# Sparse attention and a mixture-of-experts block on one core: scores and maxima in units of two heads

## The reference

```python
qkv = layernorm(x) @ w_qkv                  # 2 x 1024 x 384
q, k, v = heads(qkv)                        # 2 batches x 16 heads, 1024 x 8
s = q @ k.T / sqrt(8), -inf where key > query
att = softmax(s) @ v                        # then @ w_o, residual, layernorm, experts
```

## Time and profile before

| | us |
|---|---|
| median of 3 runs | 2053.17 (2050.89 to 2055.31) |
| the profiled execution's own span | 2056.6 |
| TensorE (PE) busy in it | 1720.3 (84%) |
| PE weight loads busy | 999.4 (49%) |
| VectorE (DVE) busy | 1287.6 (63%) |
| ScalarE (ACT) busy | 1111.6 (54%) |
| GpSimd (POOL) busy | 548.3 (27%) |

### The profile page before, as it was taken

One profiled execution on the slowest core, in us unless ns is written; L12 is line 12 of the kernel. 1 busy time (PEld: TensorE's weight loads), 2 busy tenths in 40 slices (PEclk: granted clock), 3 DMA queues, 4 the chain that ended last, 5 costly groups with the idle time before them and its releaser, 6 DMA issues.

```text
span 2056.6 us, 33763 instructions
## 1 busy us (share of the span) xinstructions
PE 1720.3 (84%) x10588; PEld 999.4 (49%) x10588; DVE 1287.6 (63%) x3053; ACT 1111.6 (54%) x2328; POOL 548.3 (27%) x479
## 2 busy tenths in 40 slices
PE   3799999699967357888987978989489999969995
PEld 1344444477754114454654545556234444447774
DVE  5677775577785665464555645533467777557777
ACT  3367777388845343434344334323237767738883
POOL 6000000000001504786656867662500000000000
PEclk9699999699987566777567768567769999969998
DMA  4111110012102142101021111120211111002110
GB/s 132 64 49 50 48 46 9 27 66 83 51 2 88 62 110 49 42 28 50 28 63 46 29 46 31 43 64 18 92 62 49 50 50 44 9 30 85 61 52 21
DMA packets 66504, 104.26 MB, mean 51 GB/s; under 512 B 19432, under 2 KB 37296, under 8 KB 63280
## 3 DMA queue, kind: packets, MB, share of 16 engines
q1 hardware_dynamic: 56720, 84.86, 12.8%
q0 software_dynamic: 8192, 16.79, 2.8%
q10 hardware_dynamic: 1456, 0.90, 0.2%
HBM read 74.80 MB, written 8.59 MB: 41 GB/s over the span
## 4 chain that ended last, share of the span: by engine, by line
PE 58%; POOL 13%; issue 10%; DVE 8%; ACT 4%; SPq 3%; DVEq 2%; DMA 1%; ACTq 0%; another core or an unknown queue 0%; POOLq 0%
PE bank L701 10%; PE bank L847 8%; PE bank L685 7%; POOL onehot L639 7%; POOL arena L620 6%; PE bank L660 6%; PE bank L837 6%; PE bank L1001 2%; PE bank L1014 2%; ACT experts L1146 1%; PE bank L662 1%; PE bank L687 1%; PE bank L1029 1%; DVE arena L1313 1%; PE bank L1017 1%
## 5 line engine op out<-in xcount | busy, mean ns | idle before, releaser
L1313 DVE TENSOR_REDUCE arena<-bank 128x1 f32<-128x512 f32 (+3 forms) x768 | 382.9, 551 | 170.1 <-PE bank L662 117.3
L1073 ACT ACTIVATE arena<-bank 128x512 f32<-128x512 f32 (+3 forms) x768 | 335.2, 493 | 144.3 <-PE bank L687 121.5
L566 POOL TENSOR_TENSOR rstd<-vareps,neghalf 128x8 f32<-128x8 f32 x14 | 23.8, 1698 | 1168.0 <-DVE vareps L1306 1168.0
L660 PE MATMUL bank<-arena 72*128 72x512 bf16 (+3 forms) x768 | 259.8, 346 | 39.1 <-DMA arena<-arena 37.0
L620 POOL DMA_INDIRECT arena<-kv_rows,IDX x256 | 250.8, 980 | 155.9 <-ACT IDX L1242 86.7
L685 PE MATMUL bank<-arena 99*128 99x512 bf16 (+3 forms) x768 | 254.4, 335 | 6.0 <-ACT arena L1079 4.3
L639 POOL TENSOR_SCALAR onehot<-XT,const 128x512 fp32r<-128x512 f16 x136 | 212.4, 1573 | 160.7 <-DMA XT<-idx_rows 76.7
L701 PE MATMUL bank<-arena 128*32 128x512 f32 (+3 forms) x1536 | 225.4, 501 | 0.0
L1683 DVE TENSOR_TENSOR HN<-bank,RT 96x512 f32<-96x512 f32 x128 | 87.3, 682 | 206.8 <-PE bank L1001 144.2
L1371 DVE TENSOR_TENSOR experts<-arena,experts 128x512 fp32r<-128x512 f32 x256 | 171.6, 689 | 71.1 <-ACT experts L1146 71.1
L1144 ACT ACTIVATE arena<-bank,bias 128x512 f32<-128x512 f32 x256 | 185.6, 725 | 46.1 <-PE bank L837 46.0
(11 more groups left out here) (247 smaller groups left out, 2592.0 us busy)
## 6 DMA issues: line engine op xcount, KB each, us to landing
arena<-wt_rows SPq DMA_DIRECT2D x16, 1024.0 KB, 4.7
arena<-q_rows SPq DMA_DIRECT2D x192, 48.0 KB
arena<-k_rows SPq DMA_DIRECT2D x192, 48.0 KB
arena<-in_L_ffn_w SPq DMA_DIRECT2D x32, 256.0 KB, 5.1
arena<-arena SPq DMA_DIRECT2D x32, 256.0 KB
XT<-idx_rows SPq DMA_DIRECT2D x8, 1024.0 KB, 4.7
arena<-kv_rows,IDX POOLq DMA_INDIRECT x256
arena<-HN SPq DMA_DIRECT2D x32, 128.0 KB, 2.4
```

Of the source, the lines that this page charges most:

```text
L660: m = pe.matmul(o[:, 0:hi - lo], QB[buf][s][0:ROWS, qt * P:(qt + 1) * P], KB[buf][s][0:ROWS, lo:hi], start=True, stop=True)
L1073: act.activation(PT[w % PT_RING][:, 0:m], bank[S_RING + w % S_RING][:, 0:m], ACT.Exp, scale=float(HD) ** -0.5)\
L1313: dve.tensor_reduce(rowmax[:, hf, s, qt:qt + 1], bank[u % S_RING][:, 0:n], AX_X, ALU.max).then_inc(max_done, 1)
```

## The change

[...] Both heads of a pair lie in one tile, head 0 in rows 0 to 34 and head 1 in rows 64 to 98, and each matmul over them is one of two, in TensorE's two row halves, into two adjoining PSUM banks (`twin`). A unit is two heads by 512 columns; 9 units make a pass where 24 did. To fill 512 columns, several blocks share a unit (`PASS1`, `PASS2`): four of the maxima units and three of the scores units have one piece, two of the maxima units are four diagonal blocks, masked by one matmul of 512 columns a head, and the others have two pieces. A maximum and an exponential are one instruction over 2 x 512 columns. Maxima of pieces go to `partial` and one more reduction joins them.

Query tiles stand in the order 0, 3, 4, 7, 1, 2, 5, 6, so that each query half has 18 blocks; the values run in 5 groups instead of 8. Scores units and maxima units alternate over one ring of three twins (banks 0 to 5): a scores unit waits for the maxima unit two before it, a maxima unit for the exponential of the unit before it. Pass 1 is for the pair two ahead. PT has 6 buffers of 1024 columns. The q and k split is one ScalarE copy and one VectorE subtraction a block. A pair's rows come by 11 DMAs (4 KB rows) instead of 13, a row of zeros among them through DRAM; GpSimd makes the two masks and clears less.

The core of the diff (behind the first part only added and unchanged lines; what they replace is in the listing above):

```diff
-NPROD = 3 * 3
+PARTS = 2
 STRIP = 32
-ROWS = NPROD * HD
-MAXROW = 96
+TILE = 64
+PRODS = PARTS * PARTS * HD
 MAXROWS = 3
+ROWS = PRODS + MAXROWS
 RING = 4
...
+QORDER = [0, 3, 4, 7, 1, 2, 5, 6]
+QPLACE = [QORDER.index(t) for t in range(TB)]
+MORDER = [0, 2, 3, 1, 4, 6, 7, 5]
+MPLACE = [MORDER.index(t) for t in range(TB)]
+MSLOTS = 5
+PASS1 = [[(4, 0, 4)], [(5, 0, 4)], [(6, 0, 4)], [(7, 0, 4)], [(3, 0, 3), (1, 0, 1)], [(7, 4, 3), (5, 4, 1)], [(2, 0, 2), (6, 4, 2)],
+         [(t, t, 1) for t in MORDER[:4]], [(t, t, 1) for t in MORDER[4:]]]
+PASS2 = [[(0, 0)], [(1, 0)], [(1, 1)], [(0, 1), (0, 7)], [(0, 2), (0, 5)], [(1, 2), (1, 6)], [(0, 3), (0, 6)], [(1, 3), (1, 5)],
+         [(0, 4), (1, 4)]]
+UNITS = len(PASS1)
+GROUPS = [(0, 1), (2, 3), (4, 5), (6, 7), (8,)]
+GROUP_OF = [g for u in range(UNITS) for g, us in enumerate(GROUPS) if u in us]
+EARLY = 4
+HALFWAY = 5
 S_RING = 3
+PT_RING = 6
+TOTAL = UNITS * PAIRS
+def first_block(g, kc):
+    return [t >= kc for t in QORDER[4 * g:4 * g + 4]].index(True)
+def places(u):
+    at, out = 0, []
+    for g, kc in PASS2[u]:
+        p = first_block(g, kc)
+        out.append((g, kc, p, at))
+        at += 4 - p
+    assert at == 4
+    return out
+def diagonals(u):
+    return [at for g, kc, p, at in places(u) if QORDER[4 * g + p] == kc]
+ROW_LOADS = 16 * (2 * (2 * PARTS + 1) + 1)
...
+        twin = [ctx.enter_context(nc.psum_tensor(f"twin{i}", [P, 2 * BANK], F32)) for i in range(4)]
+        bank = [twin[i // 2][:, i % 2 * BANK:(i % 2 + 1) * BANK] for i in range(8)]
...
+        mask_qk = sb("mask_qk_b", [P, 4, P], BF16)
+        mask_kq = sb("mask_kq_b", [P, 2, P], BF16)
...
+        qparts = view("ffn", (PARTS, TOK), F32R)
+        kparts = view("ffn", (PARTS, TOK), F32R)
...
+        QB = [view("ffn", (L,), F32R) for i in range(RING)]
+        KB = [view("ffn", (L,), F32R) for i in range(RING)]
...
+        PT = [view("ffn", (2, BANK)) for i in range(PT_RING)]
+        partial = view("ffn", (2, TB, MSLOTS))
+        rowmax = view("ffn", (2, TB))
...
+                sp.wait_ge(pv_done, PV0 + len(GROUPS) * (g + it - RING + 1))
             for s in range(2):
+                q, k = (rows[it, s] if isinstance(it, int) else rows[bass.ds(it, 1), s].rearrange("a d r t -> (a d) r t") for rows in (q_rows, k_rows))
+                for i in range(PARTS):
+                    r = TILE * s + i * PARTS * HD
+                    sp.dma_start(QB[buf][r:r + PARTS * HD, :].bitcast(F32), q[:, i, :].unsqueeze(0).broadcast_to([PARTS, HD, L]))\
+                      .then_inc(rows_loaded[buf], 16)
+                    sp.dma_start(KB[buf][r:r + PARTS * HD, :].bitcast(F32), k.rearrange("d r t -> r d t")).then_inc(rows_loaded[buf], 16)
+                sp.dma_start(QB[buf][TILE * s + PRODS:TILE * s + ROWS, :].bitcast(F32), zero_rows).then_inc(rows_loaded[buf], 16)
...
+        def pe_pass1(pe, c, it, buf, u, visit, slot):
             n = PAIRS * c + it
             if u == 0:
                 pe.wait_ge(rows_loaded[buf], ROW_LOADS * (PAIRS // RING * c + visit + 1))
+            at = 0
+            for j, (qt, k0, blocks) in enumerate(PASS1[u]):
+                for s in range(2):
+                    r = slice(TILE * s, TILE * s + ROWS)
+                    q = QPLACE[qt]
+                    m = pe.matmul(bank[2 * slot + s][:, at * P:(at + blocks) * P], QB[buf][r, q * P:(q + 1) * P],
+                                  KB[buf][r, k0 * P:(k0 + blocks) * P], start=(j == 0), stop=True, skip_group_check=True)
+                at += blocks
+            if PASS1[u][0][0] == PASS1[u][0][1]:
+                for s in range(2):
+                    m = pe.matmul(bank[2 * slot + s][:, :], ident_b[:, :], mask_qk[:, :, :].rearrange("p a q -> p (a q)"),
+                                  start=False, stop=True, skip_group_check=True)
             m.then_inc(s1_done, 1)
...
+        def pe_scores(pe, c, it, buf, u, left):
             n = PAIRS * c + it
+            m = UNITS * it + u
+            if u == 0:
                 pe.wait_ge(maxrow_ready, 2 * n + 2)
+            if left >= 2:
+                pe.wait_ge(max_done, MAX0 + TOTAL * c + m + UNITS + EARLY - 1)
+            else:
+                pe.wait_ge(max_done, MAX0 + TOTAL * c + min(m + UNITS + EARLY - 1, TOTAL))
+                pe.wait_ge(exp_done, EXP0 + TOTAL * c + m - S_RING + 1)
+            slot = 2 * u % S_RING
+            for j, (g, kc, p, at) in enumerate(places(u)):
+                for s in range(2):
+                    r = slice(TILE * s, TILE * s + ROWS)
+                    x = pe.matmul(bank[2 * slot + s][:, at * P:(at + 4 - p) * P], KB[buf][r, kc * P:(kc + 1) * P],
+                                  QB[buf][r, (4 * g + p) * P:(4 * g + 4) * P], start=(j == 0), stop=True, skip_group_check=True)
+            at = diagonals(u)
+            if at:
+                for s in range(2):
+                    cut = bank[2 * slot + s][:, :].rearrange("p (t q) -> p t q", q=P)[:, at[0]:at[-1] + 1:max(1, at[-1] - at[0]), :]
+                    x = pe.matmul(cut, ident_b[:, :], mask_kq[:, 0:len(at), :], start=False, stop=True, skip_group_check=True)
+            x.then_inc(st_done, 1)
+        def pe_next(pe, c, it, buf, m, u, visit):
+            pe.wait_ge(exp_done, EXP0 + TOTAL * c + m)
+            pe_pass1(pe, c, it, buf, u, visit, (2 * ((u + HALFWAY) % UNITS) + 1) % S_RING)
...
+            for u in GROUPS[group]:
+                for g, kc, p, at in places(u):
+                    for s in range(2):
+                        r = (2 * s + g) * STRIP
+                        m = pe.matmul(bank[6][r:r + STRIP, p * P:], VS[buf][:, s, kc, :],
+                                      PT[(UNITS * buf + u) % PT_RING][:, s, at * P:(at + 4 - p) * P], start=(kc == 0), stop=True,
+                                      skip_group_check=True)
             m.then_inc(pv_done, 1)
...
+            two, one = (buf + 2) % RING, (buf + 1) % RING
+            for u in range(HALFWAY, UNITS):
+                pe_scores(pe, c, it, buf, u, left)
+                if left >= 2:
+                    pe_next(pe, c, it + 2, two, UNITS * it + u, u - HALFWAY, visit + (buf + 2) // RING)
+                if u == HALFWAY:
+                    pe_values(pe, c, it, buf, 1)
+                if u == HALFWAY + 1 and left >= 1:
                     pe_maxrows(pe, c, it + 1)
+                if u == HALFWAY + 2:
+                    pe_values(pe, c, it, buf, 2)
+            if left == 0:
+                pe_values(pe, c, it, buf, 3)
+                pe_values(pe, c, it, buf, 4)
+                pe_outputs(pe, c, it)
...
+                x = XT[:, b * L:(b + 1) * L]
+                if k < 2:
+                    x = x.rearrange("p (j i q) -> p j i q", j=2, q=P)[:, :, k:4 - k:3 - 2 * k, :]
+                else:
+                    x = x[:, (k - 2) * BANK:(k - 1) * BANK]
+                pe.matmul(bank[4 + k][:, :], w_qkv[:, (k // 2) * D:(k // 2 + 1) * D], x, start=True, stop=True).then_inc(qk_done, 1)
...
+            for x in range(UNITS + EARLY):
+                pe.wait_ge(max_done, MAX0 + TOTAL * c + x - S_RING + 1)
+                pe_pass1(pe, c, x // UNITS, x // UNITS, x % UNITS, 0, (2 * x + 2) % S_RING)
             pe_maxrows(pe, c, 0)
+            for u in range(HALFWAY):
+                pe_scores(pe, c, 0, 0, u, PAIRS)
+                pe_next(pe, c, 1, 1, u, u + EARLY, 0)
+            pe_values(pe, c, 0, 0, 0)
...
+        def act_exp(act, c, it, buf, u):
             n = PAIRS * c + it
+            act.wait_ge(st_done, UNITS * n + u + 1)
+            old = u - PT_RING
+            act.wait_ge(pv_done, PV0 + len(GROUPS) * (n if old >= 0 else n - 1) + GROUP_OF[old % UNITS] + 1)
+            act.activation(PT[(UNITS * buf + u) % PT_RING].rearrange("p s n -> p (s n)"), twin[2 * u % S_RING][:, :], ACT.Exp,
+                           scale=float(HD) ** -0.5).then_inc(exp_done, 1)
+        def act_maxrow(act, c, it, buf, s):
             act.wait_ge(mt_done, PAIRS * c + it + 1)
+            act.activation(QB[buf][TILE * s + PRODS:TILE * s + ROWS, :], bank[7][:, :].bitcast(BF16)[s * STRIP:s * STRIP + MAXROWS, :],
+                           ACT.Copy).then_inc(maxrow_ready, 1)
...
+                act_exp(act, c, it, buf, u)
+                if left >= 1 and u - HALFWAY - 1 in (0, 1):
+                    act_maxrow(act, c, it + 1, one, u - HALFWAY - 1)
             if left >= 1:
+                for u in range(2):
+                    act_exp(act, c, it + 1, one, u)
...
+            slot = (2 * (u + HALFWAY) + 1) % S_RING
+            scores = twin[slot][:, :]
+            flat = partial[:, :, :, :].rearrange("p s t j -> p s (t j)")
+            if len(PASS1[u]) == 1:
+                qt = PASS1[u][0][0]
+                to = flat[:, :, MSLOTS * MPLACE[qt] + (2 if qt == 5 else 0)]
+                dve.tensor_reduce(to, scores.rearrange("p (s k) -> p s k", s=2), AX_X, ALU.max).then_inc(max_done, 1)
+                return
+            t0 = MPLACE[PASS1[u][0][0]]
```

(17 more changed lines are left out.)

251 lines of the change are left out of this document (79 added, 172 removed).

## The result

The changed kernel takes 2156.04 to 2163.35 us (three executions) beside 2052.03 of the kernel before on the same chip: the ratio is 1.052, 95% interval 1.049 to 1.055, so it is slower by 5.2%. The forecast was 2019.

The account below looks back on a forecast made before the run. TensorE was taken to be full at 18.12 us a pair; 15.5 of work plus 1.9 of waits made 17.4, a gain of 17 us per attention, 34 for both: 2053 - 34 = 2019 us, range 1965 to 2118.

Parts of the forecast that it names:

- 13 pairs x 17.4: Steady pairs of each attention after the start at the low clock: 13 at 17.4 us, 226 us, at full clock.
- the clock falls: Rival: emptier TensorE drops to 1.2 GHz, 28 us a pair; a third of pairs so gives 2118; chance 0.22.
- The sum at 2.4 GHz: One steady pair: TensorE's work 15.5 us plus 1.9 of handover waits, 17.4 against 18.12 before.
- small pieces cost as f32: Rival: f32r pieces of 128 columns take 0.213 us each; a pair 18.7, total 2053, no change; chance 0.1.
- not side by side: Rival: f32r matmuls of the two row halves don't run together; a pair 21 us, total 2113; chance 0.08.
- Values: Values matmuls of a pair: longest column group falls from 26 to 18 blocks, 3.9 us with gaps between passes.
- Waits: TensorE's handover waits on ScalarE and VectorE in a steady pair, 1.9 us in sum.
- (a): ScalarE's three exponentials and two maxrow copies delay the next pair's unit 0 by 0.6 us, the maxima unit behind by 0.4.
- TensorE still the longest engine, with waits beside it: The forecast case itself: TensorE longest, 1.9 us of handover waits, 1990 to 2045 us; chance 0.45.
- (b): Outputs copy waits for the last values group, unit 2's exponential queues behind it on ScalarE; a maxima unit 0.7 us late.
- (c): VectorE's chain and outputs precede the next pair's first maximum; scores unit 7 waits 0.7 us, of which 0.25 stays.
- Around the steady part: Start and end of each attention: faster q and k split and fewer row DMAs start TensorE 5 us earlier.

Follow-up runs that it names:

- the kernel with the burst in the middle: The changed kernel with 16 dense full-array bf16 matmuls of 512 columns once in each attention, between pair 7 and pair 8: 2107.97 and 2217.89 us.

## Why the prediction was wrong

**The step that failed** is the term "13 pairs x 17.4" at the full clock, for both attentions. In the second one these 13 distances took 355.7 us instead of 226, at a granted clock of 0.50. The first rival, "the clock falls", had named it, with the right price, and was given 0.22. Its pair at 1.2 GHz was worked out as 28 us and measured 27.36; its premise that three such pairs of the 28 eat the gain was right. (Its columns add up to 10.4 us, not 10.2; nothing hangs on that.) Wrong were two things. I took a third of the steady pairs where it was a half: every pair of one attention. And I took the low clock for something that happens in passing, in the stretches with waits. In the rows it is a state that lasts: both attentions begin at 1.2 GHz, and TensorE must get out of it. In the kernel before the clock rose at 85.0 and at 1525.4 us, before its first steady pair; I read "1.00" in the earlier trace rows and didn't ask how it got there. Against the kernel before, 13 distances of 27.36 instead of 18.14 (119.9 us) and the last two, 36.8 instead of 31.1, are the 125.6 us that turned 25.4 ahead into 100.2 behind.

The Trainium skill's passage on short idles while PSUM buffers cycle (TensorE: Matmul & The Clock Gate, A second HAM failure mode: psum-queue depth-cycling) has the clock oscillate. The kernels with a few more columns do that; the changed kernel itself doesn't, in its profile the clock didn't change between 87.6 and 353.9 us of the first attention, nor in 355.7 us of the second.

**The sum at 2.4 GHz** held in its total: 17.4 us a pair forecast, own range 16.4 to 18.4, 16.8 measured. Its terms, against the rows above:

- Row halves, f32r: two heads' 512 columns take 0.43 with open load (0.107) and change (0.10), so 0.22 a unit; the halves run side by side. Eight pieces of 128 take 0.55 with the change, 0.45 without, and not 0.9: the rivals "small pieces cost as f32" and "not side by side" are out.
- A mask and its change 0.21, as written. At 2.4 GHz the 0.10 a change is right; in the old kernel an inserted tiny matmul with its two changes cost 0.175.
- Values: four groups of 1.00 and one of 0.57, 4.6 us, where 3.9 and ten changes at about 0.10 make 4.9; near.
- Waits: TensorE is marked idle 0.88 us a pair, where 1.9 was written. Not all waits show in the marked idle time (its busy time has the way through the array in it), so how much of the 1.9 there was is not shown. None of the marked waits is for a copy of the maxima, step (a)'s first.
- "TensorE still the longest engine, with waits beside it": half right. By taking away 16 changes and 7 open loads (2.35 us by the sum) the pair fell by 0.4 only, while a relief of ScalarE by 0.8, in a kernel with these masks, brought 0.5. I had given the handovers (a), (b) and (c) 1.0, 0.7 and 0.25. In the kernels with masks in row halves (a), ScalarE's exponentials and copies ahead of the next pair, is on the path; (b) was not taken apart; (c), the wait for VectorE's first maximum, is worth nothing there: with the 9 reductions nearly halved it is gone, and 16.4 stays. In the changed kernel itself no run takes them apart.
- Around the steady part: 5 us were expected at the start. ScalarE's split did get faster: the first row load was issued at 39.72 instead of 43.55 us, but TensorE's first unit started at 56.84 against 57.69, released by a DMA: the 11th load was issued at 47.38 and was what it waited for, 9.5 us later, where the kernel before has 4.0 (53.73 to 57.69). The step that was missing is who is late next: the landing of the loads, not their issue. The first closing copy came at 99.2 against 98.6.
- The last two pairs took 15.5 and 9.5 us (12 + 6 forecast, 17.1 and 14.1 before).

**What I had named as signs** came out so: clock 1.00 between 110 and 270 us, yes; fives in the attention slices, yes, in the other attention, which that sign had not covered; the fourfold units took 0.45 and not 0.9; the copy of the maxima as releaser of the next pair's unit 0, no.

**What stays open.** Why the first attention of the changed kernel rises (at 87.6 and 88.5 us in its two profiles) and the second doesn't, with the same instructions in it; the first isn't safe either, since in the kernel with the burst in the middle it stays at 27.36 us for seven pairs before the burst. And why pairs of 28.2 us and of 25.74 us came up within two or three when 83 of 27.36 didn't. The runs show that hardly a column is needed for it; they don't show whether it is the length of the pair, the place of its gaps or the added matmuls themselves, and a cause is not shown. Nor was it tried to start an attention at 2.4 GHz with its waits taken out.

## What to carry to other kernels

Sum a change of TensorE's work at both clocks, and ask of each stage how it gets from the low clock to the high one: if the pattern at 1.2 GHz is bound by TensorE and full of changes of tiling and open loads, a stage can stay at the low clock from end to end, and a gain of 1.3 us a pair becomes a loss of 9. A few dense matmuls (0.3 to 0.4 us a pair) were worth some 110 us, at the thin place and 10 us away from it alike, because they brought the low attention up. Look also where in a step the clock falls: a fixed distance behind a landmark names a place to fill, which moved the falls here. Before matmuls are put into a wait, see what stands on either side of them: between two row-half units they bring two changes of tiling. A profile's 1.00 tells that the clock was high in that execution, not that the pattern holds it.

## What the runs showed of the hardware

- Both clocks can last under one and the same pattern: 27.36 us for seven pairs before a burst of 5 us, 16.7 for five behind it, in one attention.
- A pair at 1.2 GHz is 1.63 times as long as at 2.4 (27.36/16.8), not twice: changes of tiling keep their time (0.10 us each, 29 a pair), and the waits of the 2.4 GHz pair (0.88 us marked) are gone.
- Full-array masks between row-half matmuls cost 0.21 us for 0.11 of columns; in the row halves 0.10.
- 48 tiny row-half matmuls a pair in a bf16 kernel with full rows make its clock fall and rise (27.5 and 44.1 us a pair); 24 don't (22.3 throughout).
- A full-array matmul of 512 columns costs 0.42 us between two row-half units, 0.22 behind a full-array mask, and nothing behind the mask that is followed by a wait.
